# TransformerGate: eight reciprocals and a spreading copy in place of a reciprocal over 512 columns

## What is computed

```
def local_attention(q, k, v):                  # b 2, h 8, n 1024, d 64
    sim = jnp.einsum('bhwid,bhwjd->bhwij', bq, bk)
    sim = jnp.where(mask, -jnp.finfo(sim.dtype).max, sim)
    attn = jax.nn.softmax(sim, axis=-1)        # exp / sum over 128 keys
    out = jnp.einsum('bhwij,bhwjd->bhwid', attn, bv)

def _layer(x, ...):
    q, k, v = split(shift_token(x) @ wqkv)     # l2norm, rotary on q and k
    x = x + local_attention(q, k, v) @ wo
    h = layernorm(shift_token(x)) @ w1 + b1
    a, g = split(h)
    x = x + (a * gelu(g)) @ w2 + b2
```

## Time and profile before

| | |
|---|---|
| median of 3 runs | 5250.49 us (5248.57 to 5253.02) |
| the profiled execution's own time | 5250.05 us |
| its span in the trace | 5248.7 us |
| mean granted TensorE clock | 0.938 |
| busy PE, DVE, ACT, POOL over the span | 4576.9, 3218.1, 2501.5, 2314.1 us |
| the 32 `invert` operations | 3.34 us each, the first from 1203.6, the last from 1660.1 us |

### The profile page before, as it was taken

The page is one execution under the profiler, slowest core; times in us unless marked ns, Lnnn a source line. Parts: engine busy times, 40 slices in busy tenths (PEclk is TensorE's granted clock), DMA queues, the critical chain, the costliest instruction groups (busy, mean ns, idle before and its releaser), DMA issues. The chain is left out here.

```text
span 5248.7 us, 68779 instructions
## 1 busy us (share of the span) xinstructions
PE 4576.9 (87%) x27376; PEld 2234.3 (43%) x27376; DVE 3218.1 (61%) x4144; ACT 2501.5 (48%) x3813; POOL 2314.1 (44%) x1323
## 2 busy tenths in 40 slices
PE   5999999977776778786789999996799999999997
PEld 3444444445554333333332222223455555555554
DVE  4756565637776677763178777745366665666563
ACT  2444444445554455552246666661244445444443
POOL 0455555558652388781100000000056666666675
PEclk8999999988998799997879999997799999999998
DMA  0000000010110000000000000000000000000000
GB/s 32 3 3 3 3 3 3 3 37 25 29 28 15 3 2 1 2 1 23 3 1 1 2 2 1 1 1 9 10 3 3 3 1 3 3 3 1 3 1 9
DMA packets 61954, 36.81 MB, mean 7 GB/s; under 512 B 36308, under 2 KB 53888, under 8 KB 61376
## 3 DMA queue, kind: packets, MB, share of 16 engines
q1 hardware_dynamic: 61632, 32.41, 2.4%
HBM read 22.03 MB, written 1.05 MB: 4 GB/s over the span
## 5 line engine op out<-in xcount | busy, mean ns | idle before, releaser
L793 DVE TENSOR_REDUCE L_part<-banks 128x2 f32<-128x1024 f32 (+2 forms) x1600 | 1882.2, 1189 | 997.6 <-PE banks L644 856.7
L778 ACT ACTIVATE L_weights<-banks 128x1024 f32<-128x1024 f32 (+1 forms) x1600 | 1581.4, 1001 | 1052.3 <-PE banks L676 840.8
L702 PE MATMUL banks<-L_weights,L_V 128*32 128x512 f32 (+3 forms) x6400 | 1499.4, 604 | 5.4 <-ACT L_weights L778 3.3
L1000 POOL TENSOR_TENSOR L_wsum<-L_wsum,L_weights 128x1024 f32<-128x1024 f32 (+1 forms) x448 | 985.3, 2199 | 55.6 <-ACT L_weights L778 2.8
L983 POOL TENSOR_TENSOR L_wsum<-L_wsum,L_two 128x1024 f32<-128x1024 f32 x240 | 570.9, 2379 | 855.4 <-DVE L_two L967 852.5
L702 PEld LDWEIGHTS banks<-L_weights,L_V 128*64 128x64 f32 (+1 forms) x6400 | 283.9, 123 | 460.8 <-issue 399.0
L676 PE MATMUL banks<-L_QH,L_KH 64*128 64x512 f32 (+3 forms) x1664 | 432.6, 453 | 17.9 <-issue 10.2
L2509 POOL MEMSET F_xr<- 128x16 f32 x1 | 0.1, 126 | 936.6 <-POOLq L97 936.6
L644 PE MATMUL banks<-L_KH,L_QH 64*128 64x512 f32 (+3 forms) x1664 | 373.9, 430 | 31.7 <-ACT L_weights L778 17.7
L676 PE MATMUL banks<-L_QL,L_KH 64*128 64x512 f32 (+3 forms) x1664 | 373.0, 382 | 0.0
L676 PE MATMUL banks<-L_QH,L_KL 64*128 64x512 f32 (+3 forms) x1664 | 372.9, 381 | 0.0
(11 more groups left out here) (445 smaller groups left out, 6034.4 us busy)
## 6 DMA issues: line engine op xcount, KB each, us to landing
F_early<-F_V SPq DMA_DIRECT2D x63, 128.0 KB, 2.4
F_tab<-xpos SPq DMA_DIRECT2D x8, 512.0 KB, 4.5
F_h<-L_ffn_h_w SPq DMA_DIRECT2D x2, 1024.0 KB, 7.1
F_wqkv<-L_ffn_wqkv SPq DMA_DIRECT2D x2, 768.0 KB
L_cos<-rope_cos SPq DMA_DIRECT2D x1, 1024.0 KB, 4.9
L_sin<-rope_sin SPq DMA_DIRECT2D x1, 1024.0 KB, 6.9
out<-X SPq DMA_DIRECT2D x1, 1024.0 KB, 5.1
F_z<-F_x SPq DMA_DIRECT2D x32, 31.8 KB
```

The source lines that it names most:

```text
L702: mm = pe.e.matmul(O[r, c:BANK], self.V[g % 2][:, kt, h, :], self.W[x % self.NW][:, y, c:BANK], start=kt < starts, stop=kt >= tiles - starts)
L778: act.e.activation(self.W[x % self.NW][:, :, c:BANK], self.banks(it)[:, :, c:BANK], ACT.Exp, scale=self.scale).then_inc(self.exped, 1)
L793: dve.e.tensor_reduce(self.part[n % 3][:, pr, j, p, :], self.banks(it)[:, :, 0:wide], AX.X, ALU.max).then_inc(self.mx_read, 1)
L1000: pool.e.tensor_tensor(acc[:, :, c:BANK], acc[:, :, c:BANK], W[:, :, c:BANK], ALU.add).then_inc(self.summed, 1)
```

## The change

`rden` becomes 8 numbers per token. VectorE first takes the reciprocal of the eight sums, as a link of `Chain` (so that the engine waits for its own result), and then copies them, each read 64 times, into a new tile `wide` of 512 columns. The wait for `over` of the step before (the last reader of the 512 columns) moves behind the reciprocal. PE turns `wide`. Nothing else is changed, neither the list nor another engine's instructions.

```
-        self.nm, self.den, self.rden = two("nm", [P, 8]), two("den", [P, 8]), sb("rden", [P, 8, 64])
+        self.nm, self.den, self.rden = two("nm", [P, 8]), two("den", [P, 8]), sb("rden", [P, 8])
+        self.wide = sb("wide", [P, 8, 64])
...
-            m = pe.e.transpose(Y[:, j * P:(j + 1) * P], self.rden[:, 2 * j:2 * j + 2, :].rearrange("p h a -> p (h a)"), self.core.ident[:, :])
+            m = pe.e.transpose(Y[:, j * P:(j + 1) * P], self.wide[:, 2 * j:2 * j + 2, :].rearrange("p h a -> p (h a)"), self.core.ident[:, :])
...
                 dve.wait_ge(self.expd, t + 1)
+                self.chain(dve.e.reciprocal(self.rden[:, :], self.den[t % 2][:, :]))
                 if t:
                     self.ymade(dve, ("over", t - 1))
-                over = self.den[t % 2][:, :].rearrange("p (h a) -> p h a", a=1).to_broadcast([P, 8, 64])
-                dve.e.reciprocal(self.rden[:, :, :], over).then_inc(self.den_made, 1)
+                dve.e.tensor_copy(self.wide[:, :, :], self.rden[:, :].rearrange("p (h a) -> p h a", a=1).to_broadcast([P, 8, 64])).then_inc(self.den_made, 1)
```

## The result

The changed kernel takes 5175.44 us (median of 4 runs, 5165.65 to 5185.61), the kernel before, timed beside it, 5249.53. The ratio is 0.9864, 95% interval 0.9834 to 0.9893: 1.4% faster. 5186 was forecast, with a range from 5172 to 5208. The profiled execution took 5168.04 us, 82 less than that of before, and this difference has to be taken apart, because not all of it is the change's.

A forecast was written before the change was run, and what follows sets the result against it. No engine is full; a loop passing between engines sets the pace, with the reciprocal on it four times a unit. Gains 6.4 + 45.6 + 9.6, plus 3.5 for clock, less 1 for lock: 64 us, 5186 from 5250.05; range 5172 to 5208.

The forecast's parts named there:

- The price of the edit: VectorE, reciprocal's start to F_x: 0.23 plus 0.35 gives 0.58 in place of 3.26, saving 2.68 us a step.
- first: First step of a unit: F_x comes 2.68 us earlier, but only 1.6 is carried on and 1.1 lost.
- second: Second step of a unit: PE and POOL wait for VectorE's work, so all 2.68 us is kept, 4.3 so far.
- third: Third step of a unit: F_x comes 7.0 us earlier, PE gains only 1.2 more, 5.5 so far; 1.5 lost.
- fourth: Fourth step of a unit: F_x 8.2 us earlier, PE's wait of 2.11 caps the gain at 2.1, 7.6 in all.
- the cap by ACT's queue: First step: ACT's exponentials, squares and copies gain about 0.65; its second root begins at 1388.35 instead of 1389.94.
- PE's wait of 1.19: Third step: PE waited only 1.19 us for F_x, so PE, ACT's squares and VectorE's sums gain 1.2 more.
- the fourth rival: PE's remaining long wait, for POOL's rotation, lowers the mean clock to 0.75: 9.3 us more work a unit, 5260; chance 0.02.
- the clock ahead of the down projection: Fourth step: closing PE's wait restores full clock, 1.4 us in each of 5 units, 7 us; half counted, 3.5.
- the lock: VectorE's copy waits for POOL's operation in flight, at most 1.26 us, in third and fourth steps; 1 us deducted.
- The ends: First unit gains 6.4 us, its first two steps only 1.1 together because POOL bounds it; last unit gains 9.6.
- the lock's rival: The copy waits about 0.8 us everywhere and delays POOL's first rotation: 25 us lost, 39 gained, 5211; chance 0.12.

The follow-up runs named there:

- The run with the two idle-filling matmuls: Kernel before, plus two useless matmuls (1.9 us) on PE in its wait ahead of the down projection: gate's length 447.6 against 456.5 us, median 5245.93, ratio 0.9999.
- the full dose: Changed kernel, reciprocal over 8 columns: gate's length 390.5 us against 456.5 before; with tensor_reduce instead of the copy 390.6, median 5180.29.
- half the dose: Changed kernel with the reciprocal over 256 columns instead of 8: gate's length 442.3, median 5222.9 us; with tensor_reduce for the copy 426.4 and 5220.61.

## Why the prediction was right

**The price of the edit.** 0.23 + 0.35 = 0.58 was the sum; reciprocal 0.19 and copy 0.43 in place of 0.204 and 0.43. The start of F_x came 0.57 us behind the reciprocal's where the copy met nothing (1437.91 to 1438.48), 0.68 where it waited a little. The line drawn through two rows held, and it holds with a stride of zero. The Trainium skill's statement that one element read again and again by a stride of zero still moves two columns a cycle (Vector Engine (DVE) Microarchitecture Reference, section 5.1, Performance modes) agrees with the trace: the copy took 0.43 us, where `tensor_reduce` took 0.69 for as many columns.

**Step by step.** Means over units two to six, start of reciprocal to the next one, taken from the two traces:

| step | before | changed | gained | forecast |
|---|---|---|---|---|
| first | 13.03 | 11.24 | 1.8 | 1.6 |
| second | 17.87 | 15.62 | 2.3 | 2.7 |
| third | 17.39 | 15.82 | 1.6 | 1.2 |
| fourth | 15.04 | 11.35 | 3.7 | 2.1, and 0.7 for the clock |
| unit | 63.33 | 54.03 | 9.3 | 7.6 and 0.7 |

The first step gave about what the cap by ACT's queue allows and the third what PE's wait of 1.19 allows, a little looser; no run tests the two caps by themselves. The second kept less than all: PE comes to its wait for POOL earlier, 4.69 us in all five units where it was 3.59 in the mean, and some of the gain goes into matmuls at half clock. The fourth gained 2.3 us where the down projection had been at full clock before (13.66 to about 11.3), against 2.1; the rest of its 3.7 is the clock. The half clock behind the wait for POOL was the mechanism of the fourth rival, at a place that it named, but a few tenths of a microsecond in size, not the 9.3 that it would have needed.

**The term that was mis-sized** is the clock ahead of the down projection. I gave it half a chance and 3.5 us, five units of 1.4 each. After the change it is at full clock in all five, 2.84 to 2.94 us. The full term was nearly right, but by two errors that cancel: before, only three of the five took 4.57 (the others 4.12 and 2.94), and each of these three got 1.6 to 1.7 us back, since 24 matmuls take 2.9 and not 3.2. In all it is 20.8 less 14.3, 6.5 us. The run with the two idle-filling matmuls shows that cause alone, 6.9 us in the fourth steps. In the second profile of the kernel before, one more of the five was at full clock and the term is 4.8 us.

**The sum.** The gate's end came 70 us earlier, 6 more than the 64 of the forecast. Of these the clock is 3, other waits in units two to seven that gave a little more 3, the last unit 1 and the lock, which cost nothing, 1; the first unit gave 2 less. Each of these is no larger than the 3.3 us by which the gate's length varies, so one pair of profiles doesn't settle them singly; the 70 is shown.

**The ends.** The first unit ended 4.4 us earlier, not 6.4, and 0.8 of this is that the gate began earlier in that profile. Its first two steps took 28.2 us instead of 27.7, where a gain of 1.1 was forecast; in the second profiles of both kernels it is 28.1 instead of 29.2, so one pair of profiles can't settle this term. The other two steps gained 4.0 instead of 5.3, with a copy of 0.84 us in one of them. The last unit gained 10.5, up to the gate's end, where 9.6 was forecast.

**The lock.** 6.2 us of waits in all (5.2 and 3.8 in the other profiles), against 0.2 x 32 = 6.4 taken from the 64-column copy. Where they fall was half wrong: I had them in the third and the fourth step. In units two to six they are in the fourth (0.44 to 0.96 us) and the first (0.53 to 1.48), while in the third the copy took 0.43 in four units and 0.50 in one. POOL stood idle in the first step before; after, in the third unit, one of its rotations began at 1303.72 and the copy of the first step at 1303.79. At the full dose they cost nothing that the gate's length shows (390.6 without them). But this was luck of place rather than a small risk: at half the dose the same lock took 16 of 30 us. The Trainium skill's rule (SBUF — State Buffer, section Who interferes with whom) agrees with these traces: copies waited, up to 1.48 us, and none of 64 `tensor_reduce` operations lasted longer than 0.69. I had put the lock's rival at 0.12, and the forecast's own sum would not have noticed a phase in which it decides.

**The total.** The median, 5175, lay 11 us below the forecast, of which 6 are the gate. For the rest the levels of the mixture stage are large enough; that they make it up was not shown. No gain of that stage belongs to the change. The forecast took the profiled execution's 5250 as the base; the kernel before in fact ran from 5232 to 5256. In the two later comparisons the changed kernel's median was 5169 and 5171, just under the range's end of 5172, beside 5242 and 5246 for the kernel before: 73 and 76 us less, as the first 74. So that the time itself fell into the range is partly luck of the base; the difference is sound.

## What to carry to other kernels

Don't multiply a saving by its count: ask in each step which wait ends next. Here 86 us on VectorE became 70 (66 between the first and the last reciprocal), and 37 at half the dose became 14. A saving on one engine can return time on another, by closing a wait behind which PE works at half clock, and an operation swapped for a shorter one can fall under a lock that the old one was free of. Read a stage's length in the profile before you credit a difference of totals: 12 of the first 82 us here came from a stage that wasn't touched.

## What the runs showed of the hardware

- The reciprocal costs 6.25 ns a column: 0.19 us for 8 columns, 1.74 for 256, 3.34 for 512 (fp32, 128 partitions).
- `tensor_reduce` over one element, with 512 columns of output, takes 0.69 us and doesn't wait for POOL.
- A copy within SBUF of 512 fp32 columns, read with a stride of zero, takes 0.43 us; with a POOL operation begun 0.07 us before it, 1.48.
- The stationary operand of a matmul can be read with a stride of zero (64 equal columns from one): the run without the copy does so in all 32 steps.
- Whether the granted clock falls behind a short wait of PE isn't decided by the wait's length alone. Behind 1.28 and 0.39 us the 24 matmuls of the down projection took 2.94 us in all five units. Behind 2.06 to 2.11 us they took more than that (4.10 to 4.57) in four of five units of the kernel before and three of five in its second profile, in all five at the half dose with the copy, and in only one of five where matmuls of no use had been added some 25 us earlier. What else decides it is open.
- A stage of continuous PE work (20 us busy of 20) can run at a granted clock of 0.50 in one execution and 1.00 in the next, with either kernel. The cause is open.
